# Products of the identity, read by nobody, in TensorE's waits of a linear attention

## The reference

```python
def _feat(x):
    return jax.nn.elu(x) + 1.0
q = layernorm(x) @ Wq + bq              # 16 heads of width 8
c = (layernorm(x) @ Wk..., Wv...) @ Wc @ We   # keys and values through a low rank
phi_q, phi_k = _feat(q), _feat(k)
a = tril(phi_q @ phi_k.T)               # 64 x 64 per head
o = (a @ v) / (a.sum(-1) + eps)
x = x + gamma * layernorm(xn + o @ Wo + bo) + beta
```

## Time and profile before

| | |
|---|---|
| median of 3 executions | 7279.12 us |
| lowest and highest | 7273.06 and 7292.24 us |
| the profiled execution's own time | 7265.86 us |
| its span, first to last instruction | 7263.9 us |
| TensorE matmuls busy | 6467.9 us, 89% |
| VectorE busy | 5358.4 us, 74% |
| ACT, POOL busy | 4050.6 us, 56%; 2821.8 us, 39% |
| mean granted TensorE clock | 0.961 of full |

### The profile page before, as it was taken

The page is one execution under the profiler, slowest core; times in us unless marked ns, Lnnn a source line. Parts: engine busy times, 40 slices in busy tenths (PEclk is TensorE's granted clock), DMA queues, the critical chain, the costliest instruction groups (busy, mean ns, idle before and its releaser), DMA issues. The chain is left out here.

```text
span 7263.9 us, 188991 instructions
## 1 busy us (share of the span) xinstructions
PE 6467.9 (89%) x74572; PEld 3955.5 (54%) x74572; DVE 5358.4 (74%) x8929; ACT 4050.6 (56%) x6024; POOL 2821.8 (39%) x1680
## 2 busy tenths in 40 slices
PE   7989987887697899989999779989899999989998
PEld 5766664443442333333333356666576667666676
DVE  7867476665556999999999856677577777768444
ACT  4556343665446777777777745455344444456433
POOL 3311175332215888888888601165022222212000
PEclk9999988999898999999999989999999999999999
DMA  1000000000101222222222100000000000000000
GB/s 29 0 22 12 10 4 8 3 3 2 15 1 56 73 75 75 73 84 76 76 77 74 52 12 13 9 31 3 12 2 2 2 2 2 2 16 14 1 0 23
DMA packets 115880, 190.02 MB, mean 26 GB/s; under 512 B 38661, under 2 KB 74746, under 8 KB 114970
## 3 DMA queue, kind: packets, MB, share of 16 engines
q1 hardware_dynamic: 112218, 183.47, 8.0%
q10 hardware_dynamic: 3264, 0.54, 0.1%
HBM read 173.87 MB, written 7.98 MB: 25 GB/s over the span
## 5 line engine op out<-in xcount | busy, mean ns | idle before, releaser
L2611 POOL TENSOR_TENSOR m_dBx<-m_dtx,m_Bs 128x1024 f32<-128x1024 f32 x515 | 1166.0, 2283 | 227.1 <-DVE m_hs L2976 185.0
L2976 DVE TENSOR_TENSOR_SCAN m_hs<-m_ps_dA,m_dBx 128x512 f32<-128x512 f32 x1030 | 1199.1, 1204 | 56.8 <-POOL m_dBx L2611 56.2
L2730 PE MATMUL m_ps_y<-m_yc,ident 128*128 128x512 f32 x2060 | 1021.2, 618 | 0.0
L2835 ACT ACTIVATE m_ps_dA<-m_dt,m_A 128x504 f32<-128x504 f32 x1030 | 682.0, 678 | 426.7 <-DVE m_hs L2976 424.1
L2107 POOL TENSOR_TENSOR a_s<-a_s,a_den 128x1024 f32<-128x1024 f32 x128 | 243.7, 1904 | 1123.9 <-DVE a_den L2153 1123.9
L2987 DVE TENSOR_TENSOR m_yc<-m_hs,m_ps_C 128x1024 f32<-128x1024 f32 x515 | 614.8, 1194 | 1.2 <-PE m_ps_C L2711 1.1
L2730 PEld LDWEIGHTS m_ps_y<-m_yc,ident 128*128 128x128 f32 x2060 | 350.0, 189 | 357.2 <-issue 357.2
L2711 PEld LDWEIGHTS m_ps_C<-m_parts,m_sel 48*128 48x128 bf16 x516 | 47.7, 92 | 567.1 <-DVE m_yc L2987 421.0
L2711 PE MATMUL m_ps_C<-m_parts,m_sel 48*128 48x512 bf16 x516 | 199.8, 387 | 176.0 <-DVE m_yc L2987 176.0
L636 POOL TENSOR_TENSOR c_kbd<-c_kf,c_hmask 128x1024 f32<-128x1024 f32 x66 | 125.0, 1894 | 503.0 <-ACT c_kf L545 485.0
L2151 DVE TENSOR_REDUCE a_den<-a_s 128x16 f32<-128x1024 f32 x128 | 156.0, 1219 | 207.2 <-ACT a_s L2058 207.2
(11 more groups left out here) (748 smaller groups left out, 15961.5 us busy)
## 6 DMA issues: line engine op xcount, KB each, us to landing
m_Bs<-BC_rows SPq DMA_DIRECT2D x258, 512.0 KB, 3.6
c_kvb<-in_ctxT SPq DMA_DIRECT2D x68, 128.0 KB, 2.1
c_kvb<-in_ctxT SPq DMA_DIRECT2D x17, 256.0 KB, 2.6
out_dram<-X SPq DMA_DIRECT2D x1, 4096.0 KB
BC_rows<-m_low SPq DMA_DIRECT2D x33, 64.0 KB, 2.7
part_rows<-m_split SPq DMA_DIRECT2D x33, 48.0 KB, 1.7
m_parts<-part_rows SPq DMA_DIRECT2D x33, 48.0 KB, 1.7
m_piece<-BC_rows SPq DMA_DIRECT2D x33, 32.0 KB, 1.6
```

The lines of the kernel that those rows point to most:

```text
L2611: return nc.gpsimd.tensor_tensor(to, one, other, ALU.mult)
L2730: last = nc.tensor.matmul(ps_y[:, m, :], C.ident[:], of[:, m, :], start=s == 0, stop=s == NS - 1)
L2835: nc.scalar.activation(seqs(ps_dA[:, h % 3, :]), seqs(dt[:, par, m, :]), ACT.Exp, scale=A[:, second, m, s:s + 1]).then_inc(decay, 1)
L2976: nc.vector.tensor_tensor_scan(hs[:, s % HS, m, :], ps_dA[:, (2 * s + m) % 3, :], dBx[:, s % BX, m, :], 0.0, ALU.mult, ALU.add).then_inc(s ...
```

## The change

A helper issues products of the identity with itself into a bank, and nobody reads them. In the linear attention they go to the 224 columns of `ps_c` that `o_acc` leaves free. They stand in seven places of TensorE's order: two and three in the set-up, two behind the first transposes, two behind the first values, two behind the second unit's transposes, five behind its projections, and, in each slot from slot 1 on, four between the scores and the wait for `out_read`, behind a new wait for `on_ready`, the one with which `turn_output` begins as well. Nothing is removed.

```diff
--- before.py
+++ after.py
@@ -95,6 +95,13 @@
 
 def bc(ap, shape):
     return ap.to_broadcast(shape)
+
+
+def fill_wait(C, bank, times):
+
+
+    for _ in range(times):
+        C.nc.tensor.matmul(bank[:, 0:P], C.ident[:], C.ident[:], start=True, stop=True)
 
 
 def load_x(C, x, constants):
@@ -907,6 +914,7 @@
         ps_s, ps_a, ps_b = ps("ps_s", [P, RG, 512]), ps("ps_a", [P, 2, UC]), ps("ps_b", [P, 512])
         ps_c, ps_t = ps("ps_c", [P, 512]), ps("ps_t", [P, 512])
         o_acc = ps_c[:, 0:UT * NH * VW].rearrange("p (t h e) -> p t h e", t=UT, e=VW)
+        unread = ps_c[:, UT * NH * VW:512]
         tiles = lambda a: a.rearrange("p (t q) -> p t q", q=P)
         t_in, t_on = ps_a[:, 0, :], ps_t[:, 0:UC]
         seqs = lambda a: a.rearrange("p (s k) -> p s k", k=S)
@@ -934,11 +942,13 @@
         def _(pe):
             pe.wait_ge(loaded, n_loaded)
             nc.tensor.matmul(ps_s[0:32, 0, 0:D], wcT[:], we[:], start=True, stop=True).then_inc(folded, 1)
+            fill_wait(C, unread, 2)
             pe.wait_ge(read, 1)
             nc.tensor.matmul(ps_s[:, 1, 0:D], wkT[:], both[:], start=True, stop=True)
             nc.tensor.matmul(ps_s[:, 2, 0:D], wvT[:], both[:], start=True, stop=True)
             nc.tensor.matmul(ps_s[:, 3, 0:1], both[:], bk32[:], start=True, stop=True)
             nc.tensor.matmul(ps_s[:, 3, D:2 * D], bv32w[:], both[:], start=True, stop=True).then_inc(folded, 1)
+            fill_wait(C, unread, 3)
             pe.wait_ge(prepared, n_prepared)
 
             def turn_rows(w, par, first=False):
@@ -1012,6 +1022,8 @@
                 pe.wait_ge(masked, w + 1)
                 scores(w + 1, 1 - u)
                 if weigh:
+                    pe.wait_ge(on_ready, w)
+                    fill_wait(C, unread, 4)
                     if project:
                         pe.wait_ge(out_read, w - 1)
                     turn_output(w - 1)
@@ -1021,10 +1033,14 @@
                     project_output(w - 1)
 
             turn_rows(0, 0, True)
+            fill_wait(C, unread, 2)
             queries_keys(0, 0)
             values(0, 0, True)
+            fill_wait(C, unread, 2)
             turn_rows(1, 1)
+            fill_wait(C, unread, 2)
             queries_keys(1, 1)
+            fill_wait(C, unread, 5)
             turn_rows(2, 0)
             scores(0, 0)
             slot(0, 0, False, False)
```

## The result

The changed kernel takes 7290.76 us in the median of 20 executions (7282.14 to 7302.79), the kernel before, run beside it, 7278.91 (7273.06 to 7293.15). The ratio is 1.0014 with a 95% interval of 1.0007 to 1.0020: slower by about 10 us. The forecast was 7257.

What follows compares the result with a forecast made beforehand. In the linear attention, VectorE was taken to bound full-clock slots and TensorE half-clock ones. Loop -20.3, tail -1.9 and set-up 0 summed to -22.2 us, against 7279.12 giving 7257; range 7243 to 7275.

Steps and rivals of the forecast that it cites:

- Set-up: Start of the linear attention: fills' cost at half clock offset by a faster clock afterwards; net 0, from +2 to -5 us.
- Loop: Linear attention's 28 slots: clock stays up, 7.74 us a slot; 22.0 us less 1.7 that remain, gain 20.3 us.
- Tail: End of the linear attention: last weighing at full clock 1.6 us, projections and transposes 0.3; gain 1.9 us.
- Sum: Whole linear attention: -20.3 for its slots, -1.9 for its end, 0 for its start; -22.2 us.
- The fills' price: Linear attention slots: eight records at 0.114 to 0.135 us each, 0.91 to 1.08 us, hidden in a 1.07 us wait.
- That the clock would hold: Linear attention's loop: fills keep TensorE at full clock, removing seven half-clock stretches, 2.9 us gained for each; main unknown.
- rival B: Linear attention's loop: clock still falls now and then; half the stretches left gives 5 us gained, 7274; chance 0.15.
- C: Linear attention: fills do not count for the clock, seven stretches and slow tail remain; +16 us, 7295; chance 0.06.
- D: Linear attention: fills lengthen half-clock slots to 12.6 us and half clock feeds itself; up to +114 us, 7393; chance 0.07.
- the sum's last: Whole program: the stage's -22.2 us set against the median of 7279.12 gives 7257, -0.30%.
- a larger change in some other stage than 5 us: Stages outside the linear attention: one of the listed signs that would show the prediction wrong.
- The rule weighed against the change: Linear attention's loop: skill page blames long idle gaps for lost clock, so no falls there and gain near 0; no chance of its own.

Runs made afterwards that it cites:

- turned_code36: Changed kernel with 36 one-column products behind the linear attention's last projection and each fill issued as two identity transposes; 7256.85 us, ratio 0.9975.
- before_code28: Kernel before, no fills, with 28 one-column products (112 instructions) behind the linear attention's last projection; 7310.93 us, ratio 1.0052.
- after_code36: Changed kernel with 36 one-column products behind the linear attention's last projection, making 256 added instructions; 7253.47 us, ratio 0.9976.
- after_late9: Changed kernel with 9 unread VectorE row-statistics operations (about 1.8 us) at the end of the linear attention; 7290.52 us, ratio 1.0024.
- after_late4: Changed kernel with 4 unread VectorE row-statistics operations (about 0.8 us) at the end of the linear attention; 7290.55 us, ratio 1.0019.
- before_late8: Kernel before with 8 unread VectorE row-statistics operations (about 1.6 us) at the end of the linear attention; 7280.41 us, ratio 1.0008.
- slots_code52: Changed kernel without the set-up's 16 fills, with 52 one-column products at the stage's end, 256 added instructions; 7255.70 us, ratio 0.9977.

## Why the prediction was wrong

**The terms of the sum were right.** Set-up: forecast 0, measured -1.4 - 0.2 = -1.6 to the fourth mask. Its rows show both sides of the account:

```profile
898.52 1.65 PE L104 MATMUL a_ps_c<-ident 128*128 128x128 f32 x6
899.96 0.63 PE L960 MATMUL a_ps_a<-ident,a_xn 128*128 128x128 f32 x2
...
916.46 1.68 PE L985 MATMUL a_ps_s<-a_qbd,a_feat 32*64 32x128 f32 x64 [4.07 <-POOL a_qbd L1157]
```

The first transposes are 0.7 us late behind three fills at half clock (899.96 for the 899.25 of the earlier trace rows), and the second scores wait for POOL; what is gained comes in the slots behind. Loop: forecast -20.3, measured 1151.84 - 932.26 = 219.6 for 28 slots against 238.7, so -19.1. Tail: forecast -1.9, measured -1.7. Sum: forecast -22.2, measured -22.4 inside the stage.

**The fills' price was right.** Eight take 1.16 us from the first start to the last end, (1.16 - 0.275) / 7 = 0.126 a record, between the 0.114 and 0.135 of the two bounds. It is covered: the slots keep their 7.75 us.

**That the clock would hold was right** (rival B did not come, C and D neither). The fills' length of dense work was more than was needed: two fills do.

**The step that failed is the sum's last,** "against 7279.12 the sum gives 7257": it put the change in every other stage at nothing, without a reason. Of the added instructions it counted the executed ones, 280 records, and never the 112 in the text. These moved the first instructions of a loop 4300 us later to the end of a 16 KB piece of code, which costs 5.2 us in each turn and 29.7 us in the two profiles, more than the 22.4 that the stage gives. The prediction named "a larger change in some other stage than 5 us" as what would make it wrong, but gave it no chance. In runs: the same change at a place of the code that leaves the later loops alone is at 0.9976, at its own place 1.0014; the difference, 0.38% or 28 us, is near the 29.7 us of the loop.

**The rule weighed against the change** (long gaps alone take the clock) was rightly refused: filling a wait of 1.1 us removed seven falls. The Trainium skill, page "TensorE: Matmul & The Clock Gate", Part 4, says that transposes do not count as products do. That they count for nothing is refuted by turned_code36: eight transposes of the identity in a slot hold the clock at 1.00 for 242.4 us, where slots without them had falls. Whether they count in full stays open, since four records of products were enough too.

**What stays open.** The focus block (1193 to 2023 us) lost 12.0 us in the profile of the changed kernel and 17.5 in that of before_code28, but 1.1 in after_code36 and 18.8 in turned_code36, whose code lies as in after_code36. So its time differs from one execution to the next by as much as any effect of the code there; no run separates them, and a share of the 49.4 us of the one profile is this scatter. That the half clock of the loop is brought on by the second wait is not shown by itself, as that wait could not be taken away alone. With it (four kernels: after, after_late9, after_late4, before_code28) a fall stands at each of the six turns, of 6.83 us but for two of 3.41. Without it falls come too, but at some turns only and of 3.41 us each: one of six in the kernel before (at 6268.81), four in before_late8, three in slots_code52. So the second wait goes with more and longer falls, and is not their only cause.

## What to carry to other kernels

An edit to one engine's instruction stream has two sizes: what it executes, and how many instructions it adds to the text ahead of every later loop. The second can cost more than the first gains; look in the profile for "issue" waits at the turns of the loops behind it, count the loads of the instruction queue on the page, and try the same edit filled up to 256 instructions before judging it. Short waits of TensorE that come regularly can be filled with unread work to keep its clock, as here; try fewer fills first: at half clock TensorE has no wait to put them in the earlier trace rows, and here two held the clock as well as four.

## What the runs showed of the hardware that was not expected

- At the turn of this loop, whose body is many pieces of code long, TensorE waits about 2 us (2.13, 1.74, 2.04) for code even in the best case, and twice (2.12 and 2.44) where the loop's first instructions lie shortly before the end of a piece.
- A fall of the clock can come back at every turn of a loop: the four profiles with the second wait have it at all six turns, in the changed kernel 153.6 us apart.
- Two fills of 4 x 0.126 / 2 = 0.25 us each in a 7.75 us slot are enough to turn a loop at 0.85 of the clock into one at 1.00.
- 112 instructions that do nothing, executed once where TensorE waits anyway, cost 38 us of 7274 (0.52%, with an interval of 0.36% to 0.69%).
